# A decoder block's second cross attention: for two of eight key tiles ScalarE writes one exponential, VectorE rounds it, GpSimd takes the low part

## The reference, cut to what matters

```
scores = jnp.einsum('bhqd,bhkd->bhqk', qh, kh) / math.sqrt(hd)      # hd = 32, Sq = 512, Sk = 1024
qi = jnp.arange(Sq)[:, None] + (Sk - Sq)
ki = jnp.arange(Sk)[None, :]
causal = ki <= qi
scores = jnp.where(causal[None, None], scores, MASKED_BIAS)
attn = jax.nn.softmax(scores, axis=-1)
out = jnp.einsum('bhqk,bhkd->bhqd', attn, vh)
...
x = _layernorm(x + _L1_xattn_ref(x, ctx_2048, ctx_2048), axis=-1)
```

## Time and profile before

| | us |
|---|---|
| median of 3 runs | 2308.58 |
| lowest and highest | 2304.91 and 2310.09 |
| the profiled execution, time | 2314.31 |
| the profiled execution, span | 2312.2 |
| PE busy | 1995.7 (86%) |
| DVE busy | 1452.0 (63%) |
| ACT busy | 1076.5 (47%) |
| POOL busy | 605.4 (26%) |

### The profile page before, as it was taken

How to read it: one execution, slowest core, us unless ns; L and a number is a source line. 1 busy time by engine, 2 the same in 40 slices (tenths; PEclk the granted TensorE clock), 3 DMA queues, 4 the chain that set the end, 5 groups by cost and what they waited for, 6 DMA issues and landing times. The chain is left out here.

```text
span 2312.2 us, 32930 instructions
## 1 busy us (share of the span) xinstructions
PE 1995.7 (86%) x11168; PEld 1201.7 (52%) x11168; DVE 1452.0 (63%) x2728; ACT 1076.5 (47%) x2150; POOL 605.4 (26%) x510
## 2 busy tenths in 40 slices
PE   6777776978999889996999999996698886699998
PEld 4454553446777567773545445453255543355553
DVE  5565565456775667766856667587699966445434
ACT  3555543222333323331635446371798893244332
POOL 3555520013332223320100101011644550132320
PEclk8999987988999889998999999997699998799999
DMA  4000003111110111104011010003700003467533
GB/s 134 24 24 1 1 1 114 37 48 46 46 45 0 58 36 46 45 0 133 21 30 43 19 36 18 0 1 65 175 1 2 1 1 109 136 184 179 145 72 88
DMA packets 95792, 125.26 MB, mean 54 GB/s; under 512 B 8926, under 2 KB 52254, under 8 KB 95662
## 3 DMA queue, kind: packets, MB, share of 16 engines
q1 hardware_dynamic: 88942, 107.79, 15.8%
q0 software_dynamic: 6720, 15.73, 3.6%
HBM read 101.68 MB, written 18.61 MB: 52 GB/s over the span
## 5 line engine op out<-in xcount | busy, mean ns | idle before, releaser
L1164 POOL TENSOR_TENSOR wl<-stage,wh 128x512 fp32r<-128x512 f32 x80 | 117.2, 1496 | 399.4 <-DVE wh L1155 399.4
L1423 POOL TENSOR_TENSOR Zl<-z,Zh 128x512 f16<-128x512 f32 x32 | 51.1, 1597 | 494.3 <-ACT Zh L1584 494.3
L1264 ACT ACTIVATE h<-PS,bup 128x512 f32<-128x512 f32 x64 | 44.2, 690 | 279.2 <-PE PS L79 279.2
L77 PE MATMUL PS<-XTh,wh 128*128 128x512 f16 x416 | 157.9, 380 | 0.5 <-DVE wl L1662 0.5
L78 PE MATMUL PS<-XTl,wh 128*128 128x512 f16 x416 | 157.9, 379 | 0.0
L79 PE MATMUL PS<-XTh,wl 128*128 128x512 f16 x416 | 157.7, 379 | 0.0
L2461 POOL TENSOR_TENSOR PTl<-P,PTh 128x512 f16<-128x512 f32 (+2 forms) x128 | 116.2, 918 | 124.6 <-ACT PTh L2633 124.5
L2632 ACT ACTIVATE P<-PS 128x512 f32<-128x512 f32 (+3 forms) x256 | 135.1, 528 | 21.7 <-PE PS L2558 19.8
L2633 ACT ACTIVATE PTh<-PS 128x512 f16<-128x512 f32 (+3 forms) x256 | 136.2, 532 | 0.0
L2648 DVE TENSOR_REDUCE M<-PS 128x1 f32<-128x640 f32 (+3 forms) x128 | 127.1, 1013 | 4.5 <-PE PS L2534 4.4
L2461 DVE TENSOR_TENSOR PTl<-P,PTh 128x512 f16<-128x512 f32 (+1 forms) x128 | 96.1, 756 | 50.0 <-ACT PTh L2633 48.7
(11 more groups left out here) (378 smaller groups left out, 5831.4 us busy)
## 6 DMA issues: line engine op xcount, KB each, us to landing
stage<-in_ffn_W SPq DMA_DIRECT2D x18, 1024.0 KB, 5.4
stage<-in_ffn_Wg SPq DMA_DIRECT2D x9, 1024.0 KB, 5.5
stage<-in_ffn_Wup SPq DMA_DIRECT2D x16, 512.0 KB, 3.9
stage<-in_ffn_Wdn SPq DMA_DIRECT2D x16, 512.0 KB, 3.6
wq<-in_attn_wq SPq DMA_DIRECT2D x4, 1024.0 KB, 5.5
C<-in_ctx SPq DMA_DIRECT2D x8, 512.0 KB, 8.8
stage<-in_ffn_Wsw SPq DMA_DIRECT2D x16, 256.0 KB, 3.6
stage<-in_attn_WV SPq DMA_DIRECT2D x16, 256.0 KB, 4.1
```

The costliest lines, as they stand in the source:

```text
L77: pe.matmul(out, a[0], b[0], start=start, stop=False, skip_group_check=True)
L1164: nc.gpsimd.tensor_tensor(piece(wl[q], ch), piece(st, ch), plain(piece(wh[q], ch)), ALU.subtract).then_inc(w_lo, 1)
```

## The change

Tiles 1 and 3 of each head are made in another way. ScalarE writes `P32` only. VectorE waits for it, rounds it to `PTh` with a copy from SBUF to SBUF (`high_part`), and counts a new semaphore `high_dve`. GpSimd waits for that and takes the low part. So ScalarE has 14 exponentials a head instead of 16. VectorE has two low parts (tiles 0 and 5) instead of four, and two rounding copies besides. GpSimd has six low parts instead of four, in the order 1, 2, 3, 4, 6, 7. The wait for a free `PTh` slot (`z_done`) goes with the copy to VectorE, and the PSUM bank of such a tile is released by one exponential instead of two.

```
-    ON_POOL = (2, 4, 6, 7)
+    ON_POOL = (1, 2, 3, 4, 6, 7)
+    HIGH_ON_DVE = (1, 3)
...
         def low_part(engine, ops, n, kt, done):
             cols = slice(first_query(kt), S)
-            engine.wait_ge(exp_done, CT * n + kt + 1)
+            if kt in HIGH_ON_DVE:
+                engine.wait_ge(high_dve, len(HIGH_ON_DVE) * n + HIGH_ON_DVE.index(kt) + 1)
+            else:
+                engine.wait_ge(exp_done, CT * n + kt + 1)
...
+                    if kt in HIGH_ON_DVE:
+                        nc.scalar.activation(P32[:, kt % SLOTS, cols], c.PS[:, 4 + i % 2, cols], ACT.Exp,
+                                             scale=SC).then_inc(exp_done, 1)
+                        continue
                     need(act, z_done, i + 1 - RING)
...
+            def high_part(n, kt):
+                i = CT * n + kt
+                dve.wait_ge(exp_done, i + 1)
+                need(dve, z_done, i + 1 - RING)
+                nc.vector.tensor_copy(PTh[:, i % RING, :], P32[:, kt % SLOTS, :]).then_inc(high_dve, 1)
...
                 for kt in range(CT):
+                    if n < N and kt in HIGH_ON_DVE:
+                        high_part(n, kt)
                     if n < N and kt not in ON_POOL:
                         low_part(dve, nc.vector, n, kt, lo_dve)
```

More of the change, by code:

```diff
@@ L2429, in phase_cross1 @@
         e_done, exp_done = sem("e_done"), sem("exp_done")
-        lo_dve, lo_pool = sem("lo_dve"), sem("lo_pool")
+        lo_dve, lo_pool, high_dve = sem("lo_dve"), sem("lo_pool"), sem("high_dve")
         z_done, z_copied, c_done = sem("z_done"), sem("z_copied"), sem("c_done")
```

## The result

The changed kernel takes 2320.67 us in the median (2315.21 to 2324.48), against 2306.74 before: a ratio of 1.0058, 95% interval 1.0032 to 1.0084, so 7 to 19 us slower. The forecast was 2311.8 with a range to 2320; the result lies just above it, between the half and the whole of rival (b).

The account below looks back on a forecast made before the run. The prediction took PE's own issue work plus two round trips through ACT as the bound. Terms +1 (26 heads), +1.6 (first head) and +0.6 (late heads) gave +3.2 us, 2311.8 on the median; range 2305 to 2320.

Parts of the forecast that it names:

- rival (b): In all heads, the path shared by DVE and POOL becomes the bound: 2323.6 us whole, 2316 half; chance 0.30.
- What bounds a plain head: Plain heads: PE's issue work plus two round trips through ACT bound them; ACT's 0.98 us relief counts as nothing.
- The price of a copy: DVE's rounding copies of tiles 1 and 3: about 0.4 to 1.0 us each.
- The first head: First head: POOL's low parts and copy 1 stand behind memsets, delaying ACT's next tile 0; +1.6 us (1 to 3).
- The granted clock: Whole stage: the clock level, 0.68 in the first two heads and 1.00 after, was expected not to change.
- Late heads: Six late heads without maxima: POOL sets the pace, +0.1 us each, +0.6 in all (-5.9 to +2.4).
- rival (a): ACT's relief counts: 2305.3 us if in late heads alone, 2300 with 0.2 in each plain head; chance 0.10.
- A gain from an earlier `z`: Heads with maxima: `z` comes earlier, of which PE waited 2.9 us in all; 1 us gained as bound.
- the +1 for the 26 heads with maxima: The 26 heads with maxima together: +1 us, bounds 1 gained to 6 lost.
- I walked one plain head: Plain head from `Zs` at 0: low part 5 ends at 7.4 or 8.2, reduction at 9.3, PE wants it at 9.35.
- a third of a microsecond on each turn: Seven turns, where no margin is left after a turn: a third of a microsecond each, 2 us in all.
- its sign of 8.2: Plain heads of 8.2 us or more, with PE waiting for `M` or ACT for POOL's `PTl`, would show rival (b).

Follow-up runs that it names:

- run 1: Changed kernel with ScalarE writing both exponentials for all tiles and no VectorE copies; GpSimd keeps six low parts; ratio 0.9992 to the kernel before.
- run 4: Kernel before, with the shift's three VectorE operations moved behind the last reduction of the head; ratio 0.9997 to the kernel before.
- run 6: Changed kernel with tile 1's copy undone and tile 3's kept; GpSimd has six low parts; ratio 0.9999 to the kernel before.
- run 7: Changed kernel with tile 3's copy undone and tile 1's kept; GpSimd has six low parts; ratio 1.0023 to the kernel before.
- run 2: Changed kernel with copies kept, but VectorE takes the low parts of tiles 1 and 3 and GpSimd four; ratio 1.0125 to the kernel before.
- run 9: Changed kernel with GpSimd's memset of KS[1] made in eight pieces in heads 2 to 9; ratio 1.0038 to the kernel before.
- run 5: Changed kernel where GpSimd waits for VectorE's low part of tile 5 before its own of tile 4; ratio 1.0024 to the kernel before.
- run 10: Changed kernel with copy 1 put ahead of low part 0 in VectorE's queue; ratio 1.0034 to the kernel before.
- run 3: Changed kernel with the shift's three VectorE operations moved behind the last reduction of the head; ratio 1.0047 to the kernel before.
- run 8: Changed kernel with the shift's three VectorE operations moved into the next head, behind copy 1; ratio 1.0066 to the kernel before.
- run 11: Changed kernel with head 0 divided as before, heads 1-25 without copies, heads 26-31 with copies and GpSimd's four low parts, shift late; ratio 0.9984 to before.
- run 12: Run 11 with the memset in pieces in heads 2 to 9 and head 0 divided as heads 1 to 25; ratio 0.9981 to the kernel before.

## Why the prediction was wrong, point by point

**What bounds a plain head: right.** ACT is relieved by 0.9 us a head (7.36 busy to 6.48) and the head does not get shorter; ACT's wait for the masked score tiles grew from 19.8 to 36.6 us. A plain head of 7.96 stands in runs 1 and 4 with all of ACT's exponentials, in runs 6 and 7 with one fewer, and in run 2 with two fewer, whatever DVE and POOL carry beside it.

**The price of a copy: right.** 636 ns in the mean and 407 at least, where 0.4 to 1.0 was given. POOL busy in a plain head is 6.26 (5.9 as the sum, 6.2 to 7 as the sign).

**The first head: right in mechanism and within its bounds,** +2.2 for +1.6 (1 to 3). ACT's tile 0 of head 1 (1653.05) came 12.67 us after the first score tile, for 9.73 before: 2.9 late, where 2.1 was given, and head 1 won 0.7 of it back. Without copies (run 1) it came 2.15 late, which is the share of GpSimd's low parts, and nothing was won back. The granted clock, expected unchanged, was the term left out: in run 9 the 1.1 us that stay go with it. Copy 1 stood under the memset as said, with PE behind the reduction:

```profile
1643.47 0.69 DVE L2465 TENSOR_TENSOR PTl<-P,PTh 128x512 f16<-128x512 f32 x1 [14.74 <-ACT PTh L2641]
1644.08 3.47 DVE L2675 CAST PTh<-P 128x512 f16<-128x512 f32 x1
```

```profile
1648.33 0.61 PE L2535 MATMUL PS<-KS,QS 96*128 96x512 f16 x1 [1.91 <-DVE M L2656]
```

The Trainium skill, page "SBUF — State Buffer", section "Who interferes with whom", has a copy in a two-port mode contend with GpSimd, and a two-input operation only with GpSimd work that reads SBUF. The trace agrees on both: beside the same memset the low part of tile 0 took its undisturbed 0.69, and the copy 3.47.

**Late heads: right,** +0.11 each for +0.1, as measured against 7.27, in the four that are regular (28 to 31). The seven pieces have +1.1 for the +0.6 of the sum, since head 27, the one after the last turn, has 7.94 for 7.25. That ACT's relief has a value there, rival (a), is shown by run 2's 7.00. The changed kernel differs from run 2 there by GpSimd's two low parts more, and has 7.38.

**A gain from an earlier `z`: right and small,** the turned head went from 8.60 to 8.44, and PE's wait for `z` from 2.9 us to 0.6.

**The step that failed is the +1 for the 26 heads with maxima; it was 6.7.** I walked one plain head from a given start and found reduction 2 ending at 9.3 where PE wanted it at 9.35, and put a third of a microsecond on each turn by estimate. The walk had a slip that hid its own warning: low part 5 behind GpSimd's low part 4, which ends at 8.0, is at 8.4 by the prediction's own price of 0.41, not at 8.2, and then the reduction ends at 9.4 to 9.5, behind 9.35. Two things were missing besides. The walk was not carried into the next head: a late low part 5 makes the reductions late, these make the next copy 1 late, and that starts GpSimd's run late, so that its low part 4 again stands where low part 5 comes. POOL's run began at 3.6 us of a plain head, not at 3.1, and low part 5 ended at 8.7, not at 7.4 or 8.2. And I did not walk the heads around a turn, where 2.0 us of shift go ahead of copy 1 and no slack is left. Of the 6.7 us, the six heads after a turn among heads 2 to 25 lost 6.1 (mostly 1.14 each), the turned heads gave 1.3 back, and the twelve plain heads lost 1.9: about 0.1 each, and 0.6 in head 21, into which VectorE's first layernorm moments fall (1823.82). The seventh turn is head 27's 0.7.

Rival (b) came nearest in time, between its half and its whole, but its condition held in part only. The two engines' turns did not become the bound everywhere, as plain heads stayed at 8.06 to 8.09, under its sign of 8.2; the maximum was late for PE in the heads after a turn, and the operation held was low part 5 rather than a copy.

That this loop, and not the amount of work on the path or the queue alone, is the cause in heads 6 to 17 is shown by cutting its links one at a time. Without the copies (run 1) four heads come down by 1.44 from the changed kernel; without the meeting of low parts 4 and 5 (run 5) 1.08; with copy 1 moved ahead of one operation, at the same work (run 10), 0.69. Moving the 2.0 us of shift about (runs 3 and 8) cuts none of them and gains at most a little. Two ends stay open: why both copies together cost 0.8 more than the sum of each alone, and why the clock rises later in the first stretch. That a plain head of the changed kernel has 8.06 to 8.09 and not 7.96 I read as the same loop, in its weaker form; no run isolates it.

## What to carry to other kernels

When work is split so that one engine's first step of an iteration waits for a second engine's queue, walk two iterations and the irregular one, not a single regular one: a delay that lands ahead of that step in the second queue comes round again. Look for the operation at the end of the iteration that shares a resource with the first engine's run. Here the order in which the work was done decided more than its amount: run 10 kept all the work and gave back 0.69 of 1.20 us. And a relief of an engine is worth what the iterations give in which that engine is the bound: here the regular late heads, where it was worth 0.27 us each, once nothing else was made late.

## What the runs showed of the hardware that was not expected

The same instructions can take a different time by what came before them. In run 9 the second group of heads with memset pieces (6 to 9) took 32.98 us with 8.78 after the turn. The next four heads have no piece any more and still took 33.12 with 8.78: low part 5 took 0.56 us in their turned head, for the changed kernel's 1.48. From the third of them on it took 1.40 and 1.55, and the next four heads had 34.12 with 9.54, the changed kernel's figures, and so it stayed. The quicker state was carried on for one group of four; no run here shows that it can last. A sum of durations per head can give only one of the two times.

A 4x512 low part of the shift, 0.68 us alone, took 1.53 when it fell into GpSimd's run (run 8, and six of seven times in runs 11 and 12), although it touches only four partitions: so few were enough for it to be held. In the same way GpSimd's memset of 32 partitions held a copy of 128 for 3.47 us, while a low part beside it kept its 0.69.

In run 2 the granted clock fell to 1.2 GHz within the stage, where PE waited 24.3 us for maxima on its weight loads, and in heads 22 to 25 (0.81) the same matmuls kept PE busy 37.01 us for 29.81 before. Whether the waits brought the clock down, no run here isolates.
